# Boundary steps of a unit begun earlier, and the loop over units turned, in an attention-then-filters kernel on one Trainium2 core

## The reference, cut to what matters

```python
A, B, V = (Wa, Wb, Wv) @ xh + (ba, bb, bv)     # xh = group norm of x, per head (64, H*W)
G = A @ softmax(B, over positions).T            # 64 x 64
x = x + G @ softmax(V, over the 64 rows)
n = group norm of x
y = up(n, 12 taps, 2x, both axes) * 4 + bias    # 266 x 266 of each 128 x 128 image
y = clip(where(y >= 0, y, 0.2 * y) * sqrt(2), -256, 256)
x = x + down(y, 12 taps, 2x, both axes)
```

## Time and profile before

| | us |
|---|---|
| median of 3 runs | 16023.16 (16018.4 to 16031.98) |
| profiled execution, whole | 16040.78 |
| its span | 16039.0 |
| PE busy | 14771.9 (92%) |
| DVE busy | 12345.0 (77%) |
| ACT busy | 11570.1 (72%) |
| POOL busy | 9299.4 (58%) |
| mean granted PE clock | 0.978 |

### The profile page before, as it was taken

How to read it: one execution, slowest core, us unless ns; L and a number is a source line. 1 busy time by engine, 2 the same in 40 slices (tenths; PEclk the granted TensorE clock), 3 DMA queues, 4 the chain that set the end, 5 groups by cost and what they waited for, 6 DMA issues and landing times.

```text
span 16039.0 us, 502759 instructions
## 1 busy us (share of the span) xinstructions
PE 14771.9 (92%) x158560; PEld 12616.3 (79%) x158560; DVE 12345.0 (77%) x27932; ACT 11570.1 (72%) x20705; POOL 9299.4 (58%) x14805
## 2 busy tenths in 40 slices
PE   7999999999999999999999999999999999999999
PEld 6788877788777887778877788777887778877788
DVE  7777777777777777777777777777877778777787
ACT  6776777767777777776777777777777777777777
POOL 5555655556555565555655556555565555655556
PEclk9999999999999999999999999999999999999999
DMA  3233222333223332233322233222332223322232
GB/s 88 67 84 96 77 64 65 82 96 78 66 64 81 96 80 65 66 79 95 83 67 64 78 93 84 66 65 76 93 86 66 65 74 93 91 64 68 69 93 51
DMA packets 1998166, 1234.09 MB, mean 77 GB/s; under 512 B 79748, under 2 KB 1931140, under 8 KB 1996804
## 3 DMA queue, kind: packets, MB, share of 16 engines
q1 hardware_dynamic: 1996804, 1217.21, 29.2%
HBM read 570.85 MB, written 268.44 MB: 52 GB/s over the span
## 4 chain that ended last, share of the span: by engine, by line
PE 50%; DVE 23%; issue 12%; ACT 8%; POOL 5%; DVEq 2%; POOLq 0%; SPq 0%; DMA 0%; ACTq 0%
PE ps L1096 49%; ACT z L653 5%; DVE xh L1010 3%; DVE nblk L836 3%; DVE yb L1039 2%; DVE t L995 2%; DVE stc L731 2%; DVE nrun L840 1%; DVE mrun L825 1%; DVE srun L824 1%; POOL yb L477 1%; POOL xb L493 1%; DVE z L1001 1%; DVE bexp L843 1%; ACT alpha L590 1%
## 5 line engine op out<-in xcount | busy, mean ns | idle before, releaser
L477 POOL TENSOR_SCALAR yb<-yb 128x532 f32<-128x532 f32 x4096 | 2588.0, 632 | 3789.9 <-DVE yb L1039 3784.3
L1096 PE MATMUL ps<-dn_t,yb 128*128 128x64 f32 (+1 forms) x32768 | 4366.1, 277 | 0.3 <-POOL yb L477 0.2
L1096 PEld LDWEIGHTS ps<-dn_t,yb 128*128 128x128 f32 x32768 | 4045.2, 194 | 36.2 <-issue 24.8
L1039 DVE SCALAR_TENSOR_TENSOR yb<-yb 128x532 f32<-128x532 f32 x4096 | 3041.7, 743 | 831.1 <-ACT yb L670 820.4
L670 ACT ACTIVATE yb<-ps,bias_b 128x532 f32<-128x532 f32 x4096 | 2880.8, 704 | 710.8 <-PE ps L1096 673.6
L1096 PE MATMUL ps<-up,xn 128*128 128x266 f16 x12288 | 2057.7, 278 | 518.0 <-DVE t L995 452.4
L638 ACT ACTIVATE t<-ps 128x266 f16<-128x266 f32 x4096 | 1577.7, 390 | 1202.4 <-PE ps L1096 1177.7
L995 DVE TENSOR_TENSOR t<-ps,t 128x266 f16<-128x266 f32 x4096 | 1724.2, 425 | 635.9 <-ACT t L638 563.4
L1096 PE MATMUL ps<-up_a,t 128*128 128x138 f16 x15360 | 2025.5, 223 | 0.1
L1096 PE MATMUL ps<-up_b,t 128*128 128x138 f16 x15360 | 2022.7, 223 | 0.0
L469 POOL TENSOR_TENSOR xh<-xh,pt 128x512 f32 (+1 forms) x1024 | 1686.5, 1647 | 518.8 <-DVE pt L898 518.8
(11 more groups left out here) (158 smaller groups left out, 28903.2 us busy)
## 6 DMA issues: line engine op xcount, KB each, us to landing
xc<-in_x SPq DMA_DIRECT2D x512, 512.0 KB, 3.8
xh<-in_x SPq DMA_DIRECT2D x480, 512.0 KB, 5.0
out<-xh SPq DMA_DIRECT2D x480, 512.0 KB, 3.4
p<-t SPq DMA_DIRECT2D x960, 128.0 KB, 3.0
t<-t SPq DMA_DIRECT2D x960, 128.0 KB, 2.4
t<-p SPq DMA_DIRECT2D x960, 128.0 KB, 2.4
xn<-in_x SPq DMA_DIRECT2D x64, 512.0 KB, 5.1
xh<-in_x SPq DMA_DIRECT2D x64, 256.0 KB, 3.0
```

Source lines behind the costliest of these rows:

```text
L477: nc.gpsimd.tensor_scalar(v, v, CLAMP, -CLAMP, ALU.min, ALU.max).then_inc(s_yc, 1)
L1039: nc.vector.scalar_tensor_tensor(v, v, SLOPE, v, ALU.mult, ALU.max).then_inc(s_lr, 1)
L1096: return nc.tensor.matmul(o, l, r, start=start, stop=stop, skip_group_check=share)
```

## The change

Six things are done together.

1. **Loop.** `units` replaces the loop: attention of unit 0, then 31 times (filters of u, attention of u + 1), then the last filters. PE and ACT now branch back after their last instruction of attention, DVE after the inner loop of the second pass (its last four blocks, `last_steps`, belong to the filters' side), POOL after `add_z` of block 30.
2. **Norm 0.** `norm0_stats` moves from image 2 to 0, the variance from 4 to 2, the scales from 6 to 4 (`norm0_weights`) and 5 (`norm0_bias`); PE's two small products and ACT's root move with them. Two links between dependent steps and two memsets are taken out of the last part. `c_stats` of the last batch move into batch 14 (four there), and SP loads the last piece of `xc` in batch 13, which so has two.
3. **Exp.** ACT evaluates exp once of a constant at image 7 of the last batch, and does `exp_block(u + 1, 0, 0)` ahead of `down_high` and `remainder_high`.
4. **Norm 1, first group.** Statistics of blocks 0 to 23 are aggregated for both groups during the last four blocks of the second pass (`early_stats`); at the end only 8 records are aggregated, and PE adds both parts with two weight matrices (`avg_a`, `avg_b`). `keep_busy(42)` becomes `keep_busy(10)`.
5. **Norm 1, second group.** `next_stats` runs ahead of the reciprocal and the first low halves; the average moves on PE from image 2 to image 0, the variance on DVE from image 2 to 0 and 1, the scales from 4 to 3, ACT's root from 3 to 2.
6. **Who does what.** DVE adds block 31 to x in place of POOL; POOL does `keep_rows` between the two halves of `norm_low_half`.

```diff
-N_NORM0 = 8
-N_SMALL = N_NORM0 + 6
+N_NORM0 = 6
+N_SMALL = N_NORM0 + 8
+EARLY = 24
+        def units(eng, attention, filters):
+            attention(0)
+            with eng.Fori(0, UNITS - 1) as u:
+                filters(u, True)
+                attention(u + 1)
+            filters(UNITS - 1, False)
 # SP
-                    if before(1) and after(1) and more:
+                    if before(1) and after(2) and more:
                         load_xc(u + 1, j + 1, 1 - par)
+                    if not after(3) and after(2) and more:
+                        wait_alone(sp, s_xc[par], 16 * (XCH // 2 * (u + 2) - 1))
+                        load_xc(u + 1, j + 2, par)
 # POOL
-                for h in range(2):
-                    norm_low_half(g, 1, h)
+                norm_low_half(g, 1, 0)
                 keep_rows(NBAT * u, 0)
+                norm_low_half(g, 1, 1)
 # ACT
-                            if i == 4:
+                            if i == 3:
                                 sqrt0(u + 1)
+                            if i == IMG - 1:
+                                act.activation(exp_at, eps, ACT.Exp)
...
+                if more:
+                    exp_block(u + 1, 0, 0)
+                down_high(g, 3)
+                remainder_high(g, zr_ps)
 # DVE
+            def early_stats(u, step):
+                for gr, st in enumerate((stc, stg)):
+                    if step == gr:
+                        link(nc.vector.bn_aggr(mva[:, gr, :], st[:, 0:EARLY, :].rearrange("p a b -> p (a b)")), N_NORM0 + N_SMALL * u + 2 + gr)
+                if step == 2:
+                    for gr in range(2):
+                        last = nc.vector.scalar_tensor_tensor(mva[:, gr, 1:2], mva[:, gr, 0:1], mva[:, gr, 0:1],
+                                                              mva[:, gr, 1:2], ALU.mult, ALU.add)
+                    last.then_inc(s_gna, 1)
...
-                steps(dve, NBLK, RING, max_v)
+                steps(dve, NBLK, RING, lambda k, r, before, after: max_v(u, k, r, before, after), ends=False)
+
+            def filters(u, more):
+                base = N_NORM0 + N_SMALL * u
+                last_steps(NBLK, RING, lambda k, r, before, after: max_v(u, k, r, before, after))
                 for k in range(2):
-                    norm_z(NBLK - 2 + k, k)
+                    norm_z(u, NBLK - 2 + k, k)
+                    if k == 1:
+                        wait_alone(dve, s_zs, NBLK * (u + 1) + ZCREDIT)
+                        xv = xh_wc[:, bass.ts(NBLK - 1, WB), :]
+                        nc.vector.tensor_tensor(xv, xv, zs_[1][:].rearrange("p w h m -> p w (h m)"), ALU.add).then_inc(s_x1, 1)
...
+                next_stats(1, 0, True)
+                dve.wait_ge(s_sq1, GROUPS * u + 1)
+                link(nc.vector.reciprocal(r1[:, 0:1], v1[:, 0:1]), base + 7)
+                link(nc.vector.tensor_tensor(nmr1[:, 0:1], nm1[:, 0, 0:1], r1[:, 0:1], ALU.mult), base + 8)
+                dve.sem_inc(s_r1, 1)
+                norm(0)
+                next_stats(1, 1, True)
+                norm_low(0)
+                norm(1)
+                norm_low(1)
...
+                        if more and after(1) and not after(2) and i % 2 == 0:
+                            dve.wait_ge(s_xc[i // 4], 16 * XCH // 2 * (u + 2))
+                            c_stats(2 * j + i // 2)
-                            if i == 2:
+                            if i == 0:
                                 norm0_stats(u + 1, tail)
-                            if i == 4:
+                            if i == 2:
                                 norm0_variance(u + 1, tail)
-                            if i == 6:
-                                norm0_scales(u + 1, tail)
+                            if i == 4:
+                                norm0_weights(u + 1, tail)
+                            if i == 5:
+                                norm0_bias(u + 1, tail)
 # PE
-                keep_busy(42)
+                keep_busy(10)
+                pe.wait_ge(s_gna, u + 1)
                 pe.wait_ge(s_gn1, GROUPS * u + 1)
-                mm(tiny[:, 0:2], avg_p[:], mvh[:, 0, :], True).then_inc(s_gn1p, 1)
+                means(tiny[:, 0:2], 0, True)
                 keep_busy(26)
...
-                            average = first and i == 2 or par and after(3) and i == 5
+                            average = first and i == 0 or par and after(3) and i == 5
```

More of the change, by code:

```diff
@@ L276, in wait_alone, with steps @@
             eng.sem_inc(s_alone, 1)
-        def steps(eng, n, unroll, step, tail=1, head=0):
+        def steps(eng, n, unroll, step, tail=1, head=0, ends=True):
             for r in range(head, unroll):
@@ L597, in exp_first, with attention @@
                 gather_c(k + RING, k)
-            def unit(u, more):
+            def attention(u):
                 def exp_b(k, r, before, after):
@@ L683, in batch @@
                         first = not before(1)
-                        if first and i == 3:
+                        if first and i == 2:
                             sqrt1(slice(1, 2), 1)
@@ L722, in _ @@
                 exp_first(0, k)
-            with act.Fori(0, UNITS - 1) as u:
-                unit(u, True)
-            unit(UNITS - 1, False)
+            units(act, attention, filters)
         @block.vector
@@ new lines, in block_stats, with max_v @@
+            def block_stats(k):
+                for gr, st in enumerate((stc, stg)):
+                    last = nc.vector.bn_stats(st[:, bass.ds(k, 1), :].rearrange("p a b -> p (a b)"),
+                                              xh[:, gr * GROUP:(gr + 1) * GROUP, bass.ts(k, WB)])
+                return last
+            def max_v(u, k, r, before, after):
+                par = r % 2
+                if before(1):
+                    value_max(u, k, par)
+                if before(2):
+                    norm_z(u, k - 2, par)
+                if before(4):
+                    block_stats(k - 4)
+                if not after(RING):
+                    early_stats(u, k + RING - NBLK)
@@ L1028, in batch @@
                         q = 1 if first else j // 2 + 2
-                        read_means = first and i == 2 or group and i == 5
-                        if first and i == 4:
+                        read_means = group and i == 5
+                        if first and i == 3:
                             next_scales(q)
@@ L1048, in batch @@
                             down_low(g, i // 2 - 1)
-                        if first and i in (1, 2) or group and i in (2, 3):
-                            for step in (range(2) if first else (i - 2,)):
-                                if first and i == 2:
-                                    next_variance(q, step)
-                                else:
-                                    next_stats(q, step, first)
+                        if group and i in (2, 3):
+                            next_stats(q, i - 2, False)
+                        if first and i < 2:
+                            next_variance(q, i)
                         if group and i in (6, 7):
@@ L1086, in unit @@
                         max_first(u + 1, k)
-            with dve.Fori(0, UNITS - 1) as u:
-                unit(u, True)
-            unit(UNITS - 1, False)
+            units(dve, attention, filters)
         @block.tensor
@@ L1209, in unit, with filters, means @@
                 z(NBLK - 1, 1)
-                keep_busy(42)
+            def filters(u, more):
+                def means(o, slot, early):
+                    if early:
+                        mm(o, avg_a[:], mva[:, slot, :], True, False)
+                    mm(o, avg_b[:], mvh[:, slot, :], not early, True).then_inc(s_gn1p, 1)
+                keep_busy(10)
+                pe.wait_ge(s_gna, u + 1)
                 pe.wait_ge(s_gn1, GROUPS * u + 1)
-                mm(tiny[:, 0:2], avg_p[:], mvh[:, 0, :], True).then_inc(s_gn1p, 1)
+                means(tiny[:, 0:2], 0, True)
                 keep_busy(26)
@@ L1307, in batch @@
                             q = 1 if first else j // 2 + 2
[L1308 to L1309 removed]
+                            average = first and i == 0 or par and after(3) and i == 5
+                            up_rows(g + 1, i, 1 - par, (lambda: group_average(q, first)) if average else None)
                         if not first or i:
@@ L1377, in _ @@
                 attend_first(0, k)
-            with pe.Fori(0, UNITS - 1) as u:
-                unit(u, True)
-            unit(UNITS - 1, False)
+            units(pe, attention, filters)
 def kernel(x, L0_conv_Wa, L0_conv_ba, L0_conv_Wb, L0_conv_bb, L0_conv_Wv, L0_conv_bv, L1_conv_bias, L1_conv_up_filter,
```

136 lines of the change are left out of this document (62 added, 74 removed).

## The result

The kernel after takes 15606.26 us (median of 4 runs, 15600.48 to 15612.23), the kernel before beside it 16024.85 (16018.4 to 16031.98): a ratio of 0.9739, 95% interval 0.9722 to 0.9756. The change saves 418 us. Forecast were 15640, in a range of 15480 to 15800. The profiled execution took 15603.86 us, 436.9 us less than before by the spans.

The account below looks back on a forecast made before the run. PE's waits on its helpers, the branch stall and the half clock were taken to bound the kernel. From 16040.78, -405 + 16 - 9 + 34, then -17, gave 15660; the median lies 17.6 lower: 15642, forecast 15640, range 15480 to 15800.

Parts of the forecast that it names:

- Unit's end: Last batch through first pass: waits for s_w and exp and the branch go, 10.5 us, mean 13.7 with clock; -405 in all.
- The clock at the unit's end: Half-clock stretches of 20.4 us in 18 units, put to the 3.07 us idle, go: 5.5 us more in each.
- Idle of 1.73 us lowered no clock: Unit's end: PE's wait for exp at 7060.66 did not lower the clock, so the remaining 1.7 us idle would not.
- The late z: End of the second pass: DVE's branch stall and two aggregations make PE 0.7 us late at its last z; bounds 0 and 4.
- Attention to filters: Last z to image 4, where the branch now lies: -3.0 us or +2.9 by clock, +0.54 per unit, +16 in 30.
- 18 to 12 shares: Attention to filters: 18 units with the 20.4 us half clock, 12 with 3.4 us, taken over because the idle time is the same.
- +16 (and -9 - 17): Attention to filters: +16 over 30 units, -9 for units 0 and 31 without a branch, -17 for clock stretches filters have doubled.
- The short-clock case: Attention to filters with the clock recovering after 3.4 us: image 4 comes 3.7 us earlier, less 0.7, so -3.0.
- The branch costs by what its place hides: Loop branch: turning removes no stall, only moves its price, which is what the new place does not hide.
- The loads: Batch 13: a second 512 KB load delays SP's third swap, +1.1 us 31 times, +34; bounds 0 and 3.1 per unit.
- the forecast sum of -381: Whole run: -405 + 16 - 9 + 34 = -364, then -17 for doubled clock stretches.
- Rival 1: Unit's end gives the whole, swaps and late z cost nothing: 510 us saved, 15510; chance 0.25.

Follow-up runs that it names:

- The four parts undone one by one: Kernel after with, singly, norm steps late, exp of block 0 late, loop turned back, second group's average late: 15779.07, 15696.47, 15689.3, 15635.37 us.
- the turn alone: Kernel before with only the loop over units turned and DVE's branch ahead of its last four second-pass blocks, 42 unread products kept: 16106.33 us, 1.0059.
- Two ways to unpair the loads: Kernel after with batch 13's second load behind the first half's swaps: 15603.76 us; or with next-unit loads begun one batch earlier: 15615.82 us.
- the loop back: Kernel after with the loop over units as it was (attention, filters, branch), all else of the change kept: 15689.3 us, 0.9799.
- the norm steps late: Kernel after with the next unit's norm steps back at images 2, 4 and 6 of the last batch: 15779.07 us, 0.9856.
- exp late: Kernel after with ACT's exp of block 0 and its table load back behind the last down_high and remainder_high: 15696.47 us, 0.9804.
- three edits together: Kernel after with DVE's branch ahead of its last twelve blocks, loads one batch earlier, and DVE's sums ahead of its copy: 15585.36 us, 0.9734.

## Why the prediction was right

The time is right, and so are the mechanisms at the unit's end. The four parts undone one by one cost 187, 104, 96 and 43 us, 430 in sum (375 by the plain medians), against the 418 that the change saves. So near a sum is in part chance: each difference carries some 27 us of noise, and the parts overlap, because the clock's share of one depends on the others. Point by point, each against what the prediction said:

- **Unit's end, right.** The wait for `s_w` went. DVE's first sum now lets PE resume 8.6 us after the last batch (forecast 8.9), T3 comes at 13.9 (14.2), T4 16.3 us after the first projection (16 to 17). Mean gain 13.45 per unit, forecast 13.2. Over the run, ends of units 0 and 31 included, -413 against -405.
- **The clock at the unit's end, right, and its cause narrowed.** Behind the last batch no half-clock stretch begins in any of the 31 unit ends; one of 17.1 us reaches in from the last batch of unit 21. By the runs, either wait (`s_w` or exp) alone or the branch alone makes at most 10.2 us in nearly all units; `s_w` and exp together make 17.1 (the turn alone, 23 units), and with the branch 20.5 (before, 17 units). The prediction put it to the 3.07 us idle. That is not refuted in full: the wait for `s_w` alone was 2.0 us in the run that tested it, 2.7 in the turn alone and 3.07 before.
- **"Idle of 1.73 us lowered no clock", wrong.** The earlier trace rows showed that wait in one unit, where the clock had just recovered. The trace of before already had three other units (2, 9 and 24) in which half clock begins 0.5 us after the same wait and lasts 6.8 us. With this wait alone the clock falls in 19 units. It did no harm to the sum, because the idle of 1.32 that was left did not lower it, but it undersized exp's part.
- **The late z, undersized:** +1.57, forecast +0.7 (bounds 0 and 4). I had counted the stall and the aggregations as one load on DVE's idle time; with the aggregations in the three blocks that are left, none is left to make the stall good.
- **Attention to filters, wrong in sign by the clock's shares.** I took the 18 to 12 shares of the old place to the new one because the idle time is the same. They don't carry over: around the last z there are 22 stretches of 6.8 us and 8 of 10.2 in the 30 units, none of 20. So +16 (and -9 - 17) became -46 by the marks (30 x -1.24, and -9 for units 0 and 31). The short-clock case had image 4 earlier by 3.7 less 0.7; measured from the last z to batch 1 is 2.8, less 1.57. What made the first rows to batch 1 shorter by 3.97 is shown only in part: the average's place is worth 0.9 to 1.4 and POOL's copy 0.26; the rest, DVE's new order ahead of the first low halves among it, was not undone by itself. "HAM oscillation" in "TensorE: Matmul & The Clock Gate" of the Trainium skill says that a burst behind a wait starts at the low clock; its example has waits for DMAs of some 3 to 5 us. The traces show it behind shorter ones at three places (1.06 for 0.60 us behind the branch, 2.07 for 1.12 behind exp's wait, 7.54 us for the 42 products), but not in every unit: in 19 of 30 behind exp's wait, in 25 of 30 behind the branch put back. What one wait costs, they show, depends on what follows it.
- **The branch costs by what its place hides, right.** "Instruction fetch mechanics" in "Runtime: NRT & Kernel Launch" of the Trainium skill says that a taken branch out of what is fetched waits for a DMA of the target page. The trace agrees: packets of instructions start in each of the 30 gaps, 3 or 4 in the kernel after, 1 to 4 before. The 30 waits stay and are no shorter (95.3 us for 73.5); only without the 10 unread products does PE's wait for DVE cover them. At the unit's end a branch costs 5.7 us with its clock; behind the last z it costs 2.7 up to the average (1.47 and 1.19, PE's and DVE's together), of which 0.67 comes back before the first rows. With 42 products behind it the average alone comes 5.07 later.
- **The loads, oversized:** +34 forecast; batch 13 +0.55 and batch 14 -0.40 make +4.5 in all. PE does wait for the swap, 17.9 us in all, of which 11.0 lie in batch 13. Two ways to unpair the loads lowered that to 2.4 and 4.1 us there, but 6.8 came in batch 14 with the first and 13.2 in batch 12 with the second. The kernel with the loop back had 10.2 us of it in batch 13 and none elsewhere. What sets these waits stays open.
- **Not forecast:** +0.73 in batches 1 to 12, where PE is at half clock for 1.7 us a unit, before for none: in 16 of the 30 units a second stretch reaches over the start of batch 1. +19 in all. That the clock makes the 0.73 is argued, not tested.

The terms by the marks: -413 - 46 + 19 + 4 = -436, the 436.9 of the spans. Against the forecast sum of -381 the error of 55 is mostly attention to filters (36) and the loads (30), both too pessimistic, less the +19. Rival 1 was right that the swaps cost next to nothing, and took the rest too high.

## What to carry to other kernels

A stall that can't be removed (here a loop's branch, on average 2.5 to 3.8 us on PE) is placed by what stands ahead of and behind it: where the engine waits for another's result anyway, and never ahead of filler that was sized for a packed engine. Moving it and resizing the filler belong together: the move alone made this kernel 0.6% slower, and within the whole change it is worth 0.5 to 0.6%. Ahead of packed TensorE work a wait costs more than its length through the clock: 1.2 us more of idle a unit cost 5.6 us with the norm steps late and 3.0 with exp late. So waits there are worth more than longer ones where TensorE waits for others. The length of half-clock stretches must be read at the new place, in all units, and not carried over from the old or from one unit. Each engine branches at its own place, and DVE's was still badly placed here, close behind it two aggregations and ahead of it the work that PE needs.

## What the runs showed of the hardware

- The branch's gap on PE differed between kernels: 2.45 us on average in the kernel before, 3.2 after, 3.4 with the loop back, 3.8 with three edits together, single ones up to 4.8. Packets of instructions start in every one of these gaps: 1 to 4 before, 3 or 4 after.
- On DVE the gap was 2.6 us before and 3.1 with the loop back, on ACT 2.0 after.
- The half clock lasted 3.4, 6.8, 10.2, 13.7, 17.1 or 20.5 us, and in the same kernel and place it differed from unit to unit.
- After idle of 1.73 us it fell in 19 of 30 units with exp late, after the 1.32 of the kernel after not once in 30. Ahead of the last z it fell in 13 of 30 units where no wait of PE in the last 12 us is over 1 us.
- DVE's add of a 128x512 block in f32 to `xh`, both in SBUF, took 1.27 us, POOL's 1.65; an aggregation of 144 numbers 0.79 us, of 48 0.37.
